# A quantised MLP and a mixture-of-experts layer on one core: quantised matrices stored with the contraction on partitions, w_down loaded and worked on first, the token weight behind the first input tile, Silu straight from PSUM

## What is computed

```python
h = tok(x)                                # 448 tokens (64 x 7), each 16 x 64 numbers of x
h = h + attn(layernorm(h))                # a ternary ("bit") MLP 512 -> 2 x 1408 -> 512
h = h + ffn(layernorm(h))                 # 32 experts, top 8, 512 -> 192 -> 512

tok:  layer_norm(x, g1, b1) @ W + b, layer_norm(.., g2, b2)      # 1024 -> 512
attn: y = bitlinear(x, w_gate, g_gate); gate, v = split(y)
      z = bitlinear(gate * sigmoid(gate) * v, w_down, g_down)
bitlinear(x, w, g):
      xn = rmsnorm(x, g)
      xq = round(xn * 127 / max|xn|) / scale                     # per token, 8-bit levels
      s  = 1 / mean|w| ;  wq = clip(round(w * s), -1, 1) / s      # one scale for a whole matrix
      return xq @ wq.T
ffn:  softmax(x @ router_w.T), top 8 of 32, sum over e of w_e * (silu(x @ wg[e]) * (x @ wu[e])) @ wd[e]
```

## Time and profile before

| | us |
|---|---|
| three timed runs | 381.52, 383.54, 388.38 (median 383.54) |
| the profiled execution, its own time | 382.91 |
| its span, first to last instruction | 381.1 |
| statistics of x(0) start (DVE L1093) | 5.63 |
| first transpose of the token stage on PE (L813) | 9.01 |
| last f32 token product ends (PE L826) | 50.13 |
| front part, up to the last expert input row of group 3 (DVE L1270) | 125.11 |
| first tile's first gate and up matmul (PE L1020) | 142.1 |
| last `y` of the loop out of PSUM (ACT L790) | 363.6 |
| last `total` for w_gate (PE L847) | 50.15 |
| a cast in the MLP (`quantise2`, DVE L1253) | 0.89 |
| a copy of transposed tokens (ACT L662, 448 columns) | 0.54 |
| an expert: gate, up and down matrix, 384 KB each | 5.5 to 6.9 from issue to landing |
| last sums of the end (DVE L1419) end | 377.75 |
| the ten store DMAs are issued (SP, ACT, L416) | 375.30 to 378.84 |

### The profile page before, as it was taken

The page is one execution under the profiler, slowest core; times in us unless marked ns, Lnnn a source line. Parts: engine busy times, 40 slices in busy tenths (PEclk is TensorE's granted clock), DMA queues, the critical chain, the costliest instruction groups (busy, mean ns, idle before and its releaser), DMA issues.

```text
span 381.1 us, 5054 instructions
## 1 busy us (share of the span) xinstructions
PE 319.9 (84%) x1259; PEld 184.4 (48%) x1259; DVE 171.9 (45%) x483; ACT 134.5 (35%) x225; POOL 149.2 (39%) x139
## 2 busy tenths in 40 slices
PE   0399978857859749999999999999999999999900
PEld 0244446634526525555555555555555555555500
DVE  2555879797878762333233223322332233232102
ACT  1128888835762401232223223322322232223200
POOL 2423452343442030434544553455345444543320
PEclk9999985997987558999999999999999999999975
DMA  7999998190007261369999999999999999999467
GB/s 201 253 326 365 337 334 226 40 338 0 2 1 231 83 181 29 66 110 262 300 316 314 313 326 318 320 313 314 320 310 306 305 332 317 312 302 278 55 127 217
DMA packets 34366, 89.56 MB, mean 235 GB/s; under 512 B 4897, under 2 KB 4897, under 8 KB 34097
## 3 DMA queue, kind: packets, MB, share of 16 engines
q1 hardware_dynamic: 24800, 67.30, 53.1%
q0 software_dynamic: 8960, 21.63, 27.4%
q10 hardware_dynamic: 592, 0.47, 0.4%
HBM read 74.37 MB, written 15.02 MB: 235 GB/s over the span
## 4 chain that ended last, share of the span: by engine, by line
PE 74%; DVE 11%; DMA 6%; ACT 4%; issue 3%; SPq 1%; POOL 0%; DVEq 0%; POOLq 0%; ACTq 0%
PE ps L1020 30%; PE ps L1041 18%; PE ps L826 8%; PE ps L1030 5%; PE ps L1010 3%; PE ps L890 2%; DMA w_t<-in_x 2%; PE ps L1049 2%; PE ps L914 2%; DVE big L1190 2%; DMA sum<-w_t,add_idx 2%; PE ps L866 1%; DMA raw<-sum 1%; DMA big<-token_rows,idx 1%; PE ps L813 1%
## 5 line engine op out<-in xcount | busy, mean ns | idle before, releaser
L599 POOL DMA_INDIRECT big<-token_rows,idx x40 | 39.5, 988 | 117.4 <-DVE idx L1358 104.7
L1408 DVE SCALAR_TENSOR_TENSOR w_t<-ps,big,w_t 128x192 f32<-128x192 f32 x40 | 16.7, 418 | 125.6 <-ACT w_t L796 125.6
L612 POOL DMA_INDIRECT sum<-w_t,add_idx x40 | 63.0, 1576 | 22.4 <-issue 13.0
L1020 PE MATMUL ps<-ring,w_t 128*128 128x384 f32 x160 | 58.7, 511 | 0.0
L1041 PE MATMUL ps<-ring,w_t 96*128 96x512 f32 x116 | 54.7, 593 | 0.5 <-DVE w_t L1413 0.5
L796 ACT ACTIVATE w_t<-ps 128x192 f32<-128x192 f32 x40 | 13.2, 330 | 108.9 <-PE ps L1020 108.9
L1020 PE MATMUL ps<-big,w_t 128*128 128x384 f32 x144 | 51.1, 498 | 0.0
L790 ACT ACTIVATE w_t<-ps 128x512 f32<-128x512 f32 x40 | 23.9, 597 | 47.6 <-PE ps L1041 47.6
L535 POOL TENSOR_TENSOR root_out<-root_in,minus_half 112x1 f32<-112x1 f32 x20 | 13.2, 660 | 69.5 <-DVE root_in L1106 69.5
L1020 PEld LDWEIGHTS ps<-ring,w_t 128*128 128x128 f32 x160 | 29.7, 196 | 20.8 <-issue 5.7
L1020 PEld LDWEIGHTS ps<-big,w_t 128*128 128x128 f32 x144 | 25.9, 189 | 17.5 <-issue 3.2
(11 more groups left out here) (165 smaller groups left out, 405.2 us busy)
## 6 DMA issues: line engine op xcount, KB each, us to landing
ring<-in_L_ffn_w_down SPq DMA_DIRECT2D x29, 384.0 KB, 5.6
ring<-in_L_ffn_w_gate SPq DMA_DIRECT2D x20, 384.0 KB, 5.5
ring<-in_L_ffn_w_up SPq DMA_DIRECT2D x20, 384.0 KB, 6.9
big<-in_L_ffn_w_gate SPq DMA_DIRECT2D x18, 384.0 KB, 5.8
big<-in_L_ffn_w_up SPq DMA_DIRECT2D x18, 384.0 KB, 6.9
big<-in_L_ffn_w_down SPq DMA_DIRECT2D x9, 384.0 KB, 5.5
big<-in_L_attn_w_gate SPq DMA_DIRECT2D x2, 1536.0 KB, 17.7
ring<-in_L_attn_w_down SPq DMA_DIRECT2D x4, 704.0 KB, 17.0
```

Of the source, the lines that this page charges most:

```text
L599: nc.gpsimd.indirect_dma_start(got[:, s, :], None, rows_dram[:, :], bass.IndirectOffsetOnAxis(ap=idx[:, s:s + 1], axis=0)).then_inc(ld_got ...
L612: nc.gpsimd.indirect_dma_start(acc_dram[n][:, :], bass.IndirectOffsetOnAxis(ap=add_idx[:, s:s + 1], axis=0), y[:, s, :], None, compute_op= ...
L1020: last = nc.tensor.matmul(dst, x_t[:, st.slot(0, 2), c, :], wg[:, :, c, :], start=c == 0, stop=c == 3)
```

## The change

In words:

- **Layout on the host.** `laid_out` hands over x as 448 contiguous rows, w_gate and w_down with the contraction on partitions, the router weight likewise, and the four vectors b, g2, b2, g_gate as one row.
- **No transposes of weights.** `transpose_w` and `sign_w` go. ACT takes the sign from SBUF, in `sign_in` (11 pieces of 128 x 1024) and `sign_down` (4 pieces). All four pieces of levels of w_down are now POOL's (`levels_down`), all 11 of w_gate DVE's.
- **w_down first.** SP loads x(0), the token weight, x(1), half of w_down, x(2), the rest, x(3), and then w_gate. ACT sums w_down's absolute values (`abs_down`) before those of w_gate.
- **Vectors.** One row of 2048 numbers is loaded and spread over 112 partitions by four matmuls with ones (`spread_row`) and four ACT copies (`spread`), in place of four broadcast loads.
- **Token product in pieces**, with transposes and `total(1)` between them.
- **No casts.** The rounding constant leaves the level in the low half of the f32, which PE transposes as f16; the ACT copy takes the offset off (a scale and a bias). The DVE instructions L1166 and L1253 go.
- **Silu** by ACT from PSUM in place of the sigmoid; DVE's `gate_part` goes.
- **Order.** Group 1 is quantised ahead of the weights, group 2 between the levels; the Silu table for the loop is loaded after the flip of the mask (L772), no longer before it.
- **Places.** x lies in `ring` (was `w_t`), the four first experts all in `ring`, loop slots in `big` and `raw`; experts 5 to 7 are loaded after the last `down_gain` and `square2`, or the last transpose of q2. The stores at the end are one DMA a group (were 10 pieces in all).

```diff
...
+            def load_x(g):
+                sp.dma_start(xt[:, g, :], x[g * G:(g + 1) * G, :]).then_inc(ld_x[g], 16)
+
+            def load_down_piece(m):
+                a, b = DOWN_PART[m], DOWN_PART[m + 1]
+                sp.dma_start(w_down_raw[:, a:b, :], wdown_v[:, a:b, :]).then_inc(ld_wdown[m], 16)
+
+            load_x(0)
+            for n in range(2):
+                sp.dma_start(raw_flat[:, n * 4 * D:(n + 1) * 4 * D],
+                             w_tok.rearrange("(p c) n -> p (c n)", c=KC)[:, n * 4 * D:(n + 1) * 4 * D]
+                             ).then_inc(ld_wtok[n], 16)
+            load_x(1)
+            load_down_piece(0)
+            load_down_piece(1)
+            load_x(2)
+            load_down_piece(2)
+            load_down_piece(3)
+            load_x(3)
+            sp.wait_ge(bc_done, 4)
...
+            def levels_down(m):
+                if m == 0:
+                    pool.wait_ge(tot_read, 1)
+                w = w_down_raw[:, DOWN_PART[m]:DOWN_PART[m + 1], :]
+                nc.gpsimd.tensor_scalar(w, w, wscale[:, 1:2], MAGIC, ALU.mult, ALU.add).then_inc(pool_level_ready, 1)
+
+            root()
+            root()
             root()
             affine(0)
-            root(2)
+            root()
+            root()
+            root()
             affine(1)
+            levels_down(0)
+            root()
             root()
             affine(2)
-            pool.wait_ge(tot_read, 2)
-            for m in range(2):
-                nc.gpsimd.tensor_scalar(w_down_raw[m], w_down_raw[m], wscale[:, 1:2], LEVEL_MAGIC, ALU.mult, ALU.add
-                                        ).then_inc(pool_level_ready, 1)
-            root(2)
+            levels_down(1)
+            root()
             affine(3)
-            root(2)
-            down_gain(0)
+            levels_down(2)
+            levels_down(3)
...
+            def spread(n):
+
+                act.wait_ge(bc_done, n + 1)
+                dst = (bias_bc, g2_bc, b2_bc, gin_bc)[n]
+                nc.scalar.activation(dst[:, :], bank(2 + n)[0:G, :], ACT.Copy).then_inc(bc_ready, 1)
...
+            def sign_in(n):
+
+                act.wait_ge(level_ready, n + 1)
+                nc.scalar.activation(w_t4[:, :, 2 * n * 128:(2 * n + 2) * 128].rearrange("p c (b q) -> p b c q", b=2),
+                                     w_in_raw[:, 2 * n:2 * n + 2, :].rearrange("p b (c q) -> p b c q", c=DC), ACT.Sign,
+                                     bias=neg_magic[:, 0:1]).then_inc(wt_ready, 1)
...
+            def sign_down(m):
+
+                act.wait_ge(pool_level_ready, m + 1)
+                a, b = DOWN_PART[m], DOWN_PART[m + 1]
+                nc.scalar.activation(wd_t[:, a:b, :], w_down_raw[:, a:b, :], ACT.Sign, bias=neg_magic[:, 0:1]
+                                     ).then_inc(wd_ready, 1)
...
-                nc.scalar.activation(swi[:, g % 2, :], bank(0, 3)[0:G, 0:I1], ACT.Sigmoid, scale=deq[:, g:g + 1]
+                nc.scalar.activation(swi[:, g % 2, :], bank(0, 3)[0:G, 0:I1], ACT.Silu, scale=deq[:, g:g + 1]
...
+            def spread_row(n):
+
+                if n == 0:
+                    pe.wait_ge(ld_vec, 16)
+                nc.tensor.matmul(bank(2 + n)[0:G, :], ones[0:1, 0:G], vec_row[:, n * D:(n + 1) * D], start=True, stop=True
+                                 ).then_inc(bc_done, 1)
...
-                    last = nc.tensor.transpose(q1t_bank(g)[:, c * G // 2:(c + 1) * G // 2].bitcast(BF16),
-                                               q1[:, g % 2, c * 128:(c + 1) * 128], ident16[0:G, 0:G])
+                    last = nc.tensor.transpose(q1t_part(g)[:, c * G // 2:(c + 1) * G // 2].bitcast(F16),
+                                               low_half(h_work[:, g % 2, c * 128:(c + 1) * 128]), ident_h[0:G, 0:G])
...
             pe.wait_ge(consts, 1)
+            for n in range(3):
+                spread_row(n)
             transpose_patch(0)
+            spread_row(3)
+            tok_product(0, 0, 6)
             transpose_patch(1)
-            tok_product(0)
+            tok_product(0, 6, 8)
+            tok_product(1, 0, 4)
             transpose_patch(2)
-            tok_product(1)
+            tok_product(1, 4, 8)
+            tok_product(2, 0, 2)
+            total(1)
+            tok_product(2, 2, 4)
             transpose_patch(3)
-            tok_product(2)
-            tok_product(3)
-            pe.wait_ge(patch_act, NG)
+            tok_product(2, 4, 8)
+            tok_product(3, 0, 4)
             transpose_q1(0)
+            tok_product(3, 4, 8)
+            transpose_q1(1)
             total(0)
-            for n in range(2):
-                transpose_w(n)
-            total(1)
-            for n in range(2, 13):
-                transpose_w(n)
             gate_product(0)
-            for n in range(13, 15):
-                transpose_w(n)
             value_product(0)
-            for n in range(15, 17):
-                transpose_w(n)
-            transpose_q1(1)
-
-            pe.wait_ge(ld_late, 32)
-            pe.wait_ge(wt_ready, 17)
-            for c in range(DC):
-                last = nc.tensor.transpose(bank(6)[:, c * NE:(c + 1) * NE], rw_raw[:, c * 128:(c + 1) * 128],
-                                           ident[0:NE, 0:NE])
-            last.then_inc(rw_done, 1)
+            transpose_q1(2)
             gate_product(1)
-            transpose_q1(2)
+            transpose_q1(3)
             value_product(1)
...
+                link(nc.vector.scalar_tensor_tensor(work, h[:, g, :], mv[:, 0, 0:1], gin_bc[:, :], ALU.subtract, ALU.mult))
+                link(nc.vector.tensor_reduce(amax[:, g:g + 1], work, AX.X, ALU.max, apply_absolute_value=True))
+                link(quant_scale(0, g, get_power(n)))
+                nc.vector.tensor_scalar(work, work, fscale[:, g:g + 1], QUANT_MAGIC, ALU.mult, ALU.add).then_inc(q1_ready, 1)
...
+            def value_part(g):
+                v = swi[:, g % 2, :]
+                dve.wait_ge(value_done, g + 1)
+                dve.wait_ge(sig_ready, g + 1)
+                nc.vector.scalar_tensor_tensor(v, bank(3, 3)[0:G, 0:I1], deq[:, g:g + 1], v, ALU.mult, ALU.mult
+                                               ).then_inc(swi_ready, 1)
 
             dve.wait_ge(consts, 1)
             norm_patch(0)
+            patch_half(0)
             norm_patch(1)
-            patch_half(0)
+            patch_half(1)
             norm_patch(2)
-            patch_half(1)
-            norm_patch(3)
-            dve.wait_ge(ld_vec, 16 * 4)
-            patch_half(2)
             token_sum(0)
             token_norm(0)
-            patch_half(3)
+            patch_half(2)
+            norm_patch(3)
+            weight_scale(1, I1 * D, 1)
+            quantise1(0)
             token_sum(1)
             token_norm(1)
-            quantise1(0)
+            patch_half(3)
+            quantise1(1)
             token_sum(2)
             token_norm(2)
             token_sum(3)
-            weight_scale(0, 2 * I1 * D)
+            token_norm(3)
+            weight_scale(0, 2 * I1 * D, 2)
             product_scale(0)
-            for n in range(4):
+            product_scale(1)
+            for n in range(8):
                 levels(n)
-            weight_scale(1, I1 * D)
-            for n in range(4, 13):
+            quantise1(2)
+            product_scale(2)
+            for n in range(8, 11):
                 levels(n)
-            quantise1(1)
-            product_scale(1)
-            token_norm(3)
-
-            def gate_part(g):
-                v = swi[:, g % 2, :]
-                dve.wait_ge(sig_ready, g + 1)
-                nc.vector.tensor_tensor(v, bank(0, 3)[0:G, 0:I1], v, ALU.mult).then_inc(gate_read, 1)
-
-            def value_part(g):
-                v = swi[:, g % 2, :]
-                dve.wait_ge(value_done, g + 1)
-                dve.wait_ge(scales_ready, g + 1)
-                dve.wait_ge(gate_read, g + 1)
-                nc.vector.scalar_tensor_tensor(v, bank(3, 3)[0:G, 0:I1], deq_sq[:, g:g + 1], v, ALU.mult, ALU.mult
-                                               ).then_inc(swi_ready, 1)
-
+            value_part(0)
+            quantise1(3)
+            product_scale(3)
+            value_part(1)
...
-            prepare(2, ACT.Silu)
-
             act.wait_ge(rank_done, 1)
             nc.scalar.activation(mask_pm[:, :], bank(7)[0:NE, 0:TOK // 2].bitcast(BF16), ACT.Identity, scale=2.0,
                                  bias=minus_one[0:NE, 0:1]).then_inc(flip_ready, 1)
+            prepare(2, ACT.Silu)
...
```

390 lines of the change are left out of this document (178 added, 212 removed).

## The result

The changed kernel has a median of **394.14 us** (394.06 to 397.43, 4 runs) against 385.96 (381.52 to 389.18, 4 runs) of the kernel before on the same chip: ratio 1.0325, 95% interval 1.0223 to 1.0426, so slower. The profiled execution took 394.06, its span is 392.3, 11.2 more than before. Runs of one kernel scatter by some 2%: the ratios compare undisturbed runs only (of the kernel before 381.52 and 383.54), so they are not the quotients of the medians, and where a profiled execution was a disturbed one (the reordered version, the same with a block, and the two parts of the change alone), only its part ahead of the loop is read.

What follows compares the result with a forecast made beforehand. PE holds 74% of the chain, mostly the unchanged tile loop, so the front part's end decides. 381.1 + 8.3 - 0.3 = 389.1 span, run 390.9, median 0.6 above, given as 391 us; range 381 to 396.

Steps and rivals of the forecast that it cites:

- Part 1: Token stage: PE stands 10 us for ACT's patch half; group 3's product ends at 57.4, before 50.13, a loss of 7.3.
- Part 2: Up to w_gate's first weight scale: ACT's third sign waits for POOL; `total` at 73.0, where it was 50.15, 22.9 lost.
- Part 3: Weights to value_part(1): value_part(0) at 91.6, value_part(1) at 101; 28 behind `total`, before 36.9, so 9 come back.
- Part 4: value_part(1) to last row: two group cycles 14.5, then 18.1 from value_part(3); end at 133.4, 8.3 later than before.
- the casts' gain: Tail from value_part(3) to the last row: two casts of 0.89 leave, with 20.8 becoming 18.1.
- Part 5: The rest: table load ahead of the flip gains nothing, loop 0, end -0.3 from one store DMA.
- the range: Whole run: 381 to 396 us, taking in the milder case and most of the slower.
- the likeliest case: Whole run: stall with the clock partly down, 389 to 394 by its chance, own range 388 to 394; chance 0.50.
- line of 2%: Whole run: 391.2 us divides within 2% of before (0.45) from slower (0.44); faster had 0.11.
- The clock as a rival: Milder rival: PE's clock does not fall, 388 us, or with quicker POOL levels too, 386; milder case's chance 0.25.
- Much slower: Rival: part 3 cold throughout, `down_gain` slows more DVE work, hops of 0.15; 395 to 397 us, chance 0.13.

Runs made afterwards that it cites:

- the reordered version: Changed kernel with its work in another order on ACT, POOL, VectorE and TensorE, nothing added or left out: 372.83 us, ratio 0.9703 to the kernel before.
- the same with a block: Reordered changed kernel plus 28 small bf16 matmuls ahead of down product 1: 371.62 us, ratio 0.9719 to the kernel before.
- the two parts of the change alone: Kernel before with Silu from PSUM and no gate_part: 380.01 us; kernel before with both token weight halves loaded behind the first x: 386.62 us.
- The first two experiments: Changed kernel with all w_down signs behind those of w_gate: 380.85 us; with only the first sign behind patch_half(3): 389.5 us.
- The second experiment: Changed kernel with only the first w_down sign moved behind patch_half(3): 389.5 us, ratio 1.013 to the kernel before.
- the blocks in the gaps: Changed kernel plus unused small matmuls in PE's waits ahead of value product 1 (70) and down product 1 (28): 392.97 us, against 397.34 unaltered.
- the second timing: Changed kernel unaltered, profiled and timed again on another chip: 397.34 us, ratio 1.0381 to the kernel before.

## Why the prediction came out as it did

**Part 1, the stall: right.** ACT waited at its first sign, PE for ACT, at the places named; PE stood 8.54 for 10: it came to the wait at 40.2, not 37.5, and was released 1.1 later than forecast, though POOL's piece took 1.55, for my 2.1. The clock cost 1.7 (5.30 for a half product), where I had 2.5. That group 3's product ended 0.3 from the forecast is luck: the late release and the cheaper clock cancel. The first two experiments show that the signs are the cause: moved away, nothing of the stall beyond 2.64 remains, and 13 us go.

**Part 2, signs before sums: right.** `total` at 72.35 for 73.0, with ACT waiting 5.35 at the third sign. The second experiment shows which of the waits weighs: 2.4 of the 12.8 up to value_part(0) hang on the first sign, which was all of part 1, and 10.4 on the other three.

**Part 3: the step that failed.** I had value_part(0) at 91.6 (90.60); my own terms for it add up to 90.7 at half clock, so 0.9 there stands in no term, and the 1.0 by which it came early isn't a reading of mine. Then I had 9.4 to value_part(1) (9.65 by its terms), which took 12.50. Of the difference the value product is 2.3 (4.71 for the 2.4 that I entered), and the transposes that stand ahead of it 0.6, which I had left out. I had weighed the clock for the last quarters of the products before, where little hangs on it, and not for the product behind PE's longest gap in this stretch, 4.7 us, though my own sum made that gap: PE had to wait for quantise1(3). I entered that product at full clock without a reason; the blocks in the gaps show that this cost 2.5.

**Part 4: cycle right, tail short.** Two cycles took 14.36 for 14.5. From value_part(3) to the last row's end it was 20.7 for 18.1: 2.2 is the clock behind a gap of 1.94 (by the blocks), and 0.4, as I read it, the copy of `q2`'s transposes that the table load, now behind the last silu, holds up (transposes done at 117.9, the copy at 118.39). So, on this reading, the casts' gain was there and the clock took it back: the term of part 3 that failed, a product behind a gap at full clock, is missing here a second time. My sum has a slip besides: 101, 14.5 and 18.1 are 133.6, not 133.4. Between 133.4 and 138.16 lie 4.8: step by step 3.1 more up to value_part(1), 2.6 more in the tail and the slip of 0.2, less 1.0 for value_part(0) and 0.1 for the cycles. The two clock terms, 2.5 and 2.2, are as large as the whole.

**Part 5.** The table load ahead of the flip gave nothing, as said. A row of the changed kernel on that: a load from 116.99 took 1.28, and the next ACTIVATE began at 118.28. The Trainium skill (ScalarE: Activation LUTs, What ACT_TABLE_LOAD costs) adds 1.38 of drain to it; the trace has no room for that. What I had not seen: 1.3 came back since the router matmuls ran at full clock here and at half before. Tail and loop came as forecast within 0.5. In all 8.3 - 0.3 = 8.0 was forecast for the span; 13.05 (last row), less 1.3 (up to the first tile) and 0.6 (loop and end), is the 11.2 that came. Another slip: 390.9 and 0.6 are 391.5, where I wrote 391.

**The chances.** 394.14 lies in the range, but outside the likeliest case's line of 2%: I gave 0.45 to within 2% and 0.44 to slower, and it was 3.25% slower. The slip of 0.5 mattered here, as the line of 2% was at 391.2. The mechanism was right, and its size short by 3, 3.2 in the span. I had written that unlisted waits only add, and raised the chance of slower by 0.05 for it. The clock as a rival had been drawn to the mild side only (that it would not fall); it should have stood on the other side too, with 2 for each further product that starts behind a gap. *Much slower* named 395 to 397 with part 3 cold, at 0.13, too little for a case whose cause stood in the rows: the second timing gave 397.34.

## What to carry to other kernels

In an in-order queue a moved call that waits holds up everything behind it: find for each new wait the releaser's own place in its queue. Work that nothing needs soon, the signs of w_down here, goes behind all that somebody waits for. With that order alone the change is 0.8% faster instead of 3% slower, and with POOL's, VectorE's and TensorE's order too it is 3% faster. And list PE's gaps in the schedule that you forecast, and give each product that starts behind one both prices, half and full clock; in this kernel half was the right one behind 8.54 and 4.7, and behind 1.93 in five profiles of six.
